# Scan mixer: the tile that VectorE weighs is turned last of a state's four, behind the second scan of the next state

## The reference

```
delta = clip(softplus(dt_raw @ W_dt), 0.001, 0.1)
dA = exp(delta * A[:, n]);  dBu = delta * u * B[:, n]
h_t = dA_t * h_(t-1) + dBu_t            # over t = 0..511
y_t = sum over n of h_t[n] * C_t[n]
out = (y + u * D) * silu(res) @ W_out
```

## Time and profile before

| What | Value |
|---|---|
| median of the runs | 3179.27 us (3177.42 to 3181.41) |
| span of the profiled execution | 3174.1 us |
| first stage in it | 0 to 983 us; scans from 83.5 to 964 us |
| busy in 0 to 983 us | TensorE 772.0, VectorE 774.8, ScalarE 714.5, GpSimd 740.4 us |
| granted TensorE clock in 0 to 983 us | 0.91 of full |

### The profile page before, as it was taken

One profiled execution on the slowest core, in us unless ns is written; L12 is line 12 of the kernel. 1 busy time (PEld: TensorE's weight loads), 2 busy tenths in 40 slices (PEclk: granted clock), 3 DMA queues, 4 the chain that ended last, 5 costly groups with the idle time before them and its releaser, 6 DMA issues.

```text
span 3174.1 us, 40169 instructions
## 1 busy us (share of the span) xinstructions
PE 2724.3 (86%) x13591; PEld 1657.4 (52%) x13654; DVE 2160.0 (68%) x3854; ACT 1618.9 (51%) x2421; POOL 1047.2 (33%) x714
## 2 busy tenths in 40 slices
PE   7778887887765699999986999966989988999999
PEld 4445554454553355555554666644444445666666
DVE  1688898888886677777633222227999985777776
ACT  3778778777872245555541111127798881112111
POOL 0788887888892222111101000012212100100000
PEclk9899999999867899999998999987999998999999
DMA  3587887788884665545605000020000002000000
GB/s 114 117 171 146 180 174 157 156 173 172 154 189 91 185 176 101 81 86 88 93 16 187 24 22 24 19 56 7 14 8 11 4 1 61 7 14 7 7 7 14
DMA packets 122344, 262.93 MB, mean 83 GB/s; under 512 B 14784, under 2 KB 76992, under 8 KB 120480
## 3 DMA queue, kind: packets, MB, share of 16 engines
q0 software_dynamic: 28000, 134.89, 20.8%
q1 hardware_dynamic: 94144, 125.47, 17.2%
HBM read 135.40 MB, written 131.20 MB: 84 GB/s over the span
## 4 chain that ended last, share of the span: by engine, by line
PE 48%; issue 7%; ACT 6%; DVE 5%; DMA 1%; SPq 0%; POOL 0%; POOLq 0%; ACTq 0%; DVEq 0%
PE PS L2375 7%; PE PS L1677 6%; PE PS L2393 6%; PE PS L1971 3%; PE PS L1699 3%; ACT Z L2113 2%; PE PS L1340 2%; PE PS L2013 2%; PE PS L1319 2%; PE PS L1322 2%; PE PS L1267 2%; PE PS L1297 2%; PE PS L1366 1%; PE PS L2031 1%; PE PS L1272 1%
## 5 line engine op out<-in xcount | busy, mean ns | idle before, releaser
L856 POOL TENSOR_TENSOR Z<-Z 128x1024 f32<-128x1024 f32 x256 | 643.8, 2712 | 124.9 <-DVE Z L757 77.9
L764 DVE TENSOR_TENSOR_SCAN Z<-PS,Z 128x1024 f32<-128x1024 f32 x256 | 576.5, 2275 | 20.7 <-ACT PS L684 11.1
L535 PE MATMUL PS<-Z 128*128 128x128 f32 x2048 | 305.2, 295 | 117.0 <-DVE Z L764 46.6
L535 PEld LDWEIGHTS PS<-Z 128*128 128x128 f32 x2048 | 251.4, 152 | 250.3 <-issue 85.1
L684 ACT ACTIVATE PS<-Z 128x511 f32<-128x511 f32 x512 | 333.2, 689 | 63.8 <-DVE Z L764 62.2
L1436 ACT ACTIVATE Z<-PS 128x512 f32<-128x512 f32 x320 | 189.2, 597 | 266.7 <-PE PS L1322 262.3
L2426 ACT ACTIVATE Z<-PS 128x512 f32<-128x512 f32 x144 | 86.0, 597 | 414.0 <-PE PS L2375 414.0
L696 ACT ACTIVATE Z<-PS,Z 128x512 f32<-128x512 f32 x378 | 246.4, 685 | 75.6 <-PE PS L535 67.2
L2375 PE MATMUL PS<-Z 128*128 128x512 f32 x576 | 274.0, 601 | 7.9 <-DVE Z L2508 7.1
L1529 DVE TENSOR_REDUCE Z<-PS 128x1 f32<-128x512 f32 (+2 forms) x384 | 182.8, 508 | 119.8 <-PE PS L1298 116.2
L2113 ACT ACTIVATE Z<-Z 128x2048 f32<-128x2048 f32 x128 | 251.2, 1998 | 25.4 <-PE PS L2013 12.9
(11 more groups left out here) (293 smaller groups left out, 4895.3 us busy)
## 6 DMA issues: line engine op xcount, KB each, us to landing
sums<-Z POOLq DMA_DIRECT2D x112, 768.0 KB, 7.9
Z<-rows_b SPq DMA_DIRECT2D x128, 256.0 KB, 4.7
Z<-scr SPq DMA_DIRECT2D x256, 128.0 KB, 5.5
rows_n<-in_L_ffn_expert_wv POOLq DMA_DIRECT2D x32, 528.0 KB, 7.5
scr<-Z SPq DMA_DIRECT2D x32, 384.0 KB
Z<-Z POOLq DMA_DIRECT2D x14, 768.0 KB, 7.2
Z<-in_L_ffn_expert_wv SPq DMA_DIRECT2D x4, 2048.0 KB, 14.9
Z<-sums SPq DMA_DIRECT2D x7, 768.0 KB, 6.2
```

Source lines behind the costliest of these rows:

```text
L535: ins = e.transpose(self.turned[i % 2][:, c * 128:(c + 1) * 128], self.h(k, c // 2)[:, c % 2, i * 128:(i + 1) * 128], ident)
L764: e.tensor_tensor_scan(h, a, h, 0.0, ALU.mult, ALU.add).then_inc(s["scan"], 1)
L856: e.tensor_tensor(self.h(k, f), self.du[b % 2][:, 2 * f:2 * f + 2, :], b3(self.Bs[k % 2], 1, [128, 2, 512]), ALU.mult).then_inc(s["hin"], 1)
```

## The change

The order of the four tiles becomes 1, 2, 3, 0 for every state but the last two of the stage. TensorE turns tiles 1 and 2 in half step 2k and tiles 3 and 0 in 2k+1; the places still alternate between the two banks, so tiles 1 and 3 use `turned[0]`, and tiles 2 and 0 use `turned[1]`. ScalarE weighs tiles 1 and 2 at 2k and tile 3 at 2k+1. VectorE weighs tile 0 at 2k+1, behind the scan (n,1). The semaphore values follow: the first place waits for ScalarE's third product of the state before, the second for VectorE's sum of the state before, the third and fourth for ScalarE's first and second product of the same state.

```diff
+    def tile_at(self, k, p):
+
+        return p if k >= 16 * NB - 2 else (p + 1) % 4
+
...
         def turn(k, f):
-            for i in (2 * f, 2 * f + 1):
-                if k >= K - 2 and not (k == K - 2 and i < 2):
-                    if i == 0:
-                        e.wait_ge(s["scan"], 2 * k + 2)
-                    e.wait_ge(s["ysum"], k + 1 if i == 2 and k == K - 2 else k + 2 if k == K - 2 else K + 1 + i)
-                elif i == 0:
+            for p in (2 * f, 2 * f + 1):
+                i = self.tile_at(k, p)
+                if p == 0:
                     e.wait_ge(s["scan"], 2 * k + 2)
-                    if k:
-                        e.wait_ge(s["yprod"], 3 * k - 1)
-                elif i == 2:
-                    e.wait_ge(s["ysum"], k + 1)
-                elif k or i == 3:
-                    e.wait_ge(s["yprod"], 3 * k if i == 1 else 3 * k + 1)
+                if k == K - 1:
+                    e.wait_ge(s["ysum"], K + 1 + p)
+                elif k == K - 2 and p >= 2:
+                    e.wait_ge(s["ysum"], k + p - 1)
+                elif p == 0 and k:
+                    e.wait_ge(s["yprod"], 3 * k)
+                elif p == 1 and k:
+                    e.wait_ge(s["ysum"], k)
+                elif p >= 2:
+                    e.wait_ge(s["yprod"], 3 * k + p - 1)
                 for c in range(4):
-                    ins = e.transpose(self.turned[i % 2][:, c * 128:(c + 1) * 128],
+                    ins = e.transpose(self.turned[p % 2][:, c * 128:(c + 1) * 128],
                                       self.h(k, c // 2)[:, c % 2, i * 128:(i + 1) * 128], ident)
                 ins.then_inc(s["turn"], 1)
...
-            for i in (2, 3) if f else (1,):
-                e.wait_ge(s["turn"], 4 * k + i + 1)
+            for i in (3,) if f else (1, 2):
+                e.wait_ge(s["turn"], 4 * k + i)
...
-            elif not f:
+            elif f:
                 first_turn(k)
 
         def first_turn(k):
             b, n = divmod(k, 16)
-            e.wait_ge(s["turn"], 4 * k + 1)
-            o, y, c = self.acc[b % 2], self.turned[0], self.ct[b % 2][:, 0, 16 + n:17 + n]
+            p = 0 if k >= K - 2 else 3
+            e.wait_ge(s["turn"], 4 * k + p + 1)
+            o, y, c = self.acc[b % 2], self.turned[p % 2], self.ct[b % 2][:, 0, 16 + n:17 + n]
```

More of the change, by code:

```diff
@@ L691, in turn @@
             b, n = divmod(k, 16)
-            for i in (2, 3) if f else (1,):
-                e.wait_ge(s["turn"], 4 * k + i + 1)
+            for i in (3,) if f else (1, 2):
+                e.wait_ge(s["turn"], 4 * k + i)
                 if i == 1 and k >= 3:
                     e.wait_ge(*self.summed(k - 3))
-                e.activation(self.pr[k % 3][:, i - 1, :], self.turned[i % 2], ACT.Copy,
+                e.activation(self.pr[k % 3][:, i - 1, :], self.turned[(i - 1) % 2], ACT.Copy,
                              scale=self.ct[b % 2][:, i, 16 + n:17 + n]).then_inc(s["yprod"], 1)
```

## The result

The changed kernel takes 3195.52 us (median of 20 runs, 3182.67 to 3205.35) against 3179.40 us of the kernel before in the same comparison: ratio 1.0045, 95% interval 1.0036 to 1.0054. That is 14 us slower by the ratio and 16 us by the medians. Forecast were 3193 us and slower. The profiled execution has a span of 3196.0 us against 3174.1; from the first scan to the last it is 896.9 us against 878.2, so 18.7 of its 21.9 us lie between those two scans of the mixer.

What follows compares the result with a forecast made beforehand. No engine was full; VectorE led with 774.8 of 983 us, its waits standing where blocks have side work. Six middle blocks (11.4 us), block 0 (1.5) and block 7 (0.7) gave +13.6 us: 3193 us, range 3176 to 3206.

Steps and rivals of the forecast that it cites:

- Undisturbed states: States without side work: two scans still start every 5.02 us; -0.1 to +0.1 us each, taken as nothing.
- State 9: At the silu: weighing leaves a gap held open by ScalarE's decays, its tile comes late behind projections; +1.7 us, bounds 0.65 to 3.2.
- State 12: At clip: the 1.7 us delay arrives, one product fewer ahead of soft gives -0.57, weighing hides ahead of minus; +1.1 us.
- State 14: At scan (14,1): the weighing comes out of the wait for decays behind norm; +0.6 us, between 0.2 and 0.9.
- State 4: Behind twelve convolution passes: state 2's weighing waits instead of state 3's, holding (4,0); +0.2 us, bounds -0.4 and +1.0.
- The blocks' sum: Whole mixer: six middle blocks at 1.9 us, block 0 at 1.5, block 7 at 0.7; together +13.6 us.
- Rival (c): Ahead of mix: TensorE idles longer and runs more at low clock, +1.5 us in each of seven blocks; 3203 us, chance 0.13.
- Rival (a): At state 9, partly state 4: scan (9,1) runs while mix and turn are awaited; some -15 us, 3164 us, chance 0.11.
- Rival (b): Whole block: idle time only moves, later waits have slack, GpSimd or a DMA sets its end; 3179 +- 6 us, chance 0.18.

Runs made afterwards that it cites:

- e1: Kernel before, with the new tile order at state 8 of each block alone: 3188.1 us, ratio 1.0029 to the kernel before.
- e7: Changed kernel with ten projection passes moved from half step 18 to 17, ahead of mix: 3220.5 us, ratio 1.0112 to the kernel before.
- e10: Changed kernel with ten projection passes moved from half step 18 to 17 and back_to_x from 20 to 19: 3192.1 us, ratio 1.0029 to the kernel before.
- e9: Kernel before with ten projection passes moved from half step 18 to 17 and back_to_x from 20 to 19: 3183.3 us, ratio 1.0003.
- e13: Changed kernel again, same instructions and order, waits worked out by a helper: 3194.7 us, ratio 1.0044 to the kernel before.
- e2: Kernel before, with the new tile order at states 2, 3 and 4 of each block alone: 3187.3 us, ratio 1.0023.
- e4: Kernel before, with the new tile order at states 0, 1, 5, 6, 7, 14 and 15 alone: 3186.7 us, ratio 1.0018.
- e11: Kernel before with ten projection passes moved to half step 17 and eight of them repeated at 18: 3179.2 us, ratio 0.9988.
- e12: Changed kernel with ten projection passes moved to half step 17 and eight repeated at 18: 3193.7 us, ratio 1.0038 to the kernel before.

## Why the prediction was right

The direction, the place and the sum held: +13.6 us forecast, +14 measured by the ratio. By its steps:

- **Undisturbed states cost nothing.** Right: (0,0) to (2,0) stays at 10.05 us in the middle blocks. (The prediction's 2 x 2.23 + 0.65 gives 5.11 and not 5.02; the pitch of the scans is 2.2 us. Nothing hangs on it.)
- **State 9.** Right in its mechanism: (9,1) is released by ScalarE after the change too, and the weighing is uncovered and waits for its tile. This is shown by e1 (that state alone brings it), by e7 (the projections stood in the way) and by e10 beside e9 (most of the cost is gone once side no longer waits). The term was sized too high: for equal mixes it is 12.8 against 11.7 (1.1 us) and 14.1 against 12.4 to 12.5 (1.6 to 1.7), not 1.7 throughout. The 0.57 us by which silu and mix were to start later, taken from one product more ahead of them, measured 0.2 (mix starts 2.7 us behind (9,0) instead of 2.5); most of the difference is that ScalarE had 0.1 us of idle time there before, and got its last convolution 0.1 us sooner.
- **State 12.** Right: -0.6 forecast for the product ahead of soft, 24.26 - 24.90 = -0.64 measured. (9,0) to (13,0) so grew by 1.06 - 0.64 = 0.4 us and not by 1.1, because state 9 was sized too high. The weighing did hide ahead of minus, which still ends with du. GpSimd, changed kernel, block 3, which answers the earlier trace rows:

```profile
528.35 4.52 POOL L851 TENSOR_TENSOR Z<-Z 128x2048 f32<-128x2048 f32 x1 [1.18 <-DVE Z L751]
```

528.35 + 4.52 = 532.87, and minus ended at 531.03 + 1.85 = 532.88. The weighing at 530.39, whose other input is in PSUM, ran at its usual 0.72 us beside du. The Trainium skill (SBUF — State Buffer, section "Who interferes with whom") says that a VectorE instruction with at most one SBUF input, outside the modes that use both ports, does not contend with GpSimd; the trace agrees.

- **State 14.** Right in place, with (14,1) waiting 1.03 us for its decays. +0.6 was forecast and the means give 17.07 - 16.43 = +0.64, but the 16.43 contains a block with low clock (17.13). The other three took 16.19 to 16.20, so the cost was 0.88 us, near the upper bound of 0.9.
- **State 4.** The wait moved from the weighing of state 3 to that of state 2, as forecast. The size of +0.2 us can't be checked: the means differ by 0.0, in a stretch that varies by over 2 us between blocks.
- **The blocks' sum.** Here the sizes were off and cancelled. Six middle blocks at 1.9 us were too high; blocks 2 to 5 lost 1.1 each. Block 0 lost 4.3 us instead of 1.5, and 3.3 of them stand between (13,0) and the next (0,0), with the low clock that e13 does not have there. The sum had no term for low clock. In the changed kernel's profile it took 4.9 us behind side in block 1 and 4.0 from (14,1) of block 0 to (2,0) of block 1, 8.9 of the 18.7 us; in e13's profile it took 4.9 of 13.2 behind side. Rival (c), more low clock, was held for an extra 1.5 us a block at mix, and mix was no slower: in blocks 1 to 6 it was slow three times before and twice in the changed kernel. It came instead behind side and at state 14, and hits only some blocks. That the total fits to 1 us is luck: terms for the order that were too large stand in for low clock that was not in the sum.
- **Rival (a), overlap,** fell as argued: the wait for tiles is 60.7 after 64.3 us, and the wait for decays takes the rest of the gap. **Rival (b)** is excluded by the interval.

What stays open: why the granted clock falls behind four waits of 1.53 us and not behind twenty others of the same length (a slow mix came ahead of two of the four, and ahead of five of the twenty); what sets the start of `back`, for which the profile shows no releasing instruction in the blocks where it is late; how the losses of e2 and e4 divide between that, the clock and the places where two orders meet.

## What to carry to other kernels

An idle gap is put down to the instruction that ended it, but it can be held open by the next one as well. Before work is moved out of a gap, look what releases the instruction behind it: here it was ScalarE 0.24 us later, so the gap stayed and the moved work became a cost. And where one engine is busy without a gap and everyone waits for it, count idle time just ahead of that stretch as part of its price, since the clock for the whole stretch may hang on it.

## What was not expected of the hardware

Moving ten passes on TensorE into an idle stretch cost more than the whole change. With some 2.4 us of idle time in four pieces ahead of side, the granted clock behind it was 0.58 in a stretch of 12.3 us, in all six blocks that have the projections, and two passes of 64x512 took 2.07 us instead of 1.12. With 0.19 and 0.92 us of idle time it stayed at 1.00. With one wait of 1.53 us, beside one of 0.19 us or behind a slow mix, it fell in four cases out of 24. The sum of the idle time does not decide alone: in e9, with 0.20, 0.33 and 0.62 us, 1.15 in all, it fell in three blocks of six, and in e11, with 1.11 us in all, in none. Adding 1.9 us of repeated passes a block made the kernel 25 us faster than without them, and 0.12% faster than the one that had neither.

The idle time ahead of mix points the same way. Where it was 2.4 to 2.9 us (blocks 1 to 6 of eight profiles), mix took 5.0 us or more in 21 of 48 blocks and 3.65 in the others. Where the moved passes left 0.3 to 0.8 us of it (e7 to e12), mix took 3.65 us in all 36 blocks.
